# Second cross attention: high and low halves of the queries as one operand, division moved to the output

## The reference, cut to what matters

```
def _L1_xattn_ref(query, key):          # query: layernorm(x), (8, 64, 512); key: ctx_4096, (8, 1601, 512)
    a = jnp.einsum('bqd,bkd->bqk', query, key)
    e = jax.nn.softmax(a, axis=-1)
    c = jnp.einsum('bqk,bkd->bqd', e, key)
    return c
x = x + _L1_xattn_ref(_layernorm(x, axis=-1), ctx_4096)
```

## Time and profile before

| | |
|---|---|
| median of 3 runs | 2887.26 us (2886.32 to 2887.83) |
| the profiled execution | 2885.73 us |
| its span, first to last instruction | 2883.7 us |
| mean granted clock of PE | 0.957 |
| PE busy | 2637.2 us (91%) |
| DVE busy | 1934.6 us (67%) |
| ACT busy | 1477.2 us (51%) |
| POOL busy | 1457.2 us (51%) |
| the changed stage | from about 2414 to 2618 us of the span |

### The profile page before, as it was taken

The page is one execution under the profiler, slowest core; times in us unless marked ns, Lnnn a source line. Parts: engine busy times, 40 slices in busy tenths (PEclk is TensorE's granted clock), DMA queues, the critical chain, the costliest instruction groups (busy, mean ns, idle before and its releaser), DMA issues. The chain is left out here.

```text
span 2883.7 us, 43660 instructions
## 1 busy us (share of the span) xinstructions
PE 2637.2 (91%) x17160; PEld 2395.3 (83%) x17160; DVE 1934.6 (67%) x2229; ACT 1477.2 (51%) x2614; POOL 1457.2 (51%) x960
## 2 busy tenths in 40 slices
PE   7999999999999999999999999989846676996788
PEld 6899999999999999999999999978722245774677
DVE  3266776676677677667766776665559996775773
ACT  3455655555566556556555655554344433442552
POOL 2344744654644555463474474320039942785752
PEclk9999999999999999999999999999959997997879
DMA  5311110110110111011011110015140003442100
GB/s 199 132 46 31 52 53 23 60 46 30 46 60 25 36 57 42 25 51 60 23 53 48 35 53 23 25 64 179 63 151 0 0 15 110 148 133 77 49 1 15
DMA packets 92982, 168.67 MB, mean 58 GB/s; under 512 B 8514, under 2 KB 57922, under 8 KB 90234
## 3 DMA queue, kind: packets, MB, share of 16 engines
q1 hardware_dynamic: 82186, 153.75, 15.9%
q10 hardware_dynamic: 10608, 12.32, 1.3%
HBM read 146.05 MB, written 19.73 MB: 57 GB/s over the span
## 5 line engine op out<-in xcount | busy, mean ns | idle before, releaser
L355 POOL TENSOR_TENSOR xa_pt_lo<-xa_st,xa_pt_hi 128x1024 fp32r<-128x1024 f32 x255 | 510.9, 2029 | 630.1 <-ACT xa_pt_hi L534 630.1
L54 PE MATMUL xa_kv_ps<-ctx_wv_hi,ctx_hi 128*128 128x256 f32 (+1 forms) x1664 | 472.7, 284 | 3.1 <-DVE xa_v_lo L614 3.1
L56 PE MATMUL xa_kv_ps<-ctx_wv_hi,ctx_lo 128*128 128x256 f32 (+1 forms) x1664 | 469.3, 282 | 0.0
L55 PE MATMUL xa_kv_ps<-ctx_wv_lo,ctx_hi 128*128 128x256 f32 (+1 forms) x1664 | 464.8, 279 | 0.0
L54 PE MATMUL xa_kv_ps<-ctx_hi,ctx_wk_hi 128*128 128x402 f32 (+1 forms) x1024 | 362.9, 354 | 2.2 <-DVEq L688 2.2
L56 PE MATMUL xa_kv_ps<-ctx_hi,ctx_wk_lo 128*128 128x402 f32 (+1 forms) x1024 | 353.7, 345 | 0.0
L55 PE MATMUL xa_kv_ps<-ctx_lo,ctx_wk_hi 128*128 128x402 f32 (+1 forms) x1024 | 353.4, 345 | 0.0
L614 DVE TENSOR_TENSOR xa_v_lo<-xa_kv_ps,xa_v_hi 128x512 fp32r<-128x512 f32 (+1 forms) x224 | 146.3, 653 | 264.7 <-ACT xa_v_hi L507 263.7
L54 PEld LDWEIGHTS xa_kv_ps<-ctx_wv_hi,ctx_hi 128*128 128x128 f32 (+1 forms) x1664 | 305.6, 184 | 4.2 <-DVE xa_v_lo L614 3.3
L55 PEld LDWEIGHTS xa_kv_ps<-ctx_wv_lo,ctx_hi 128*128 128x128 f32 (+1 forms) x1664 | 307.8, 185 | 0.8
L56 PEld LDWEIGHTS xa_kv_ps<-ctx_wv_hi,ctx_lo 128*128 128x128 f32 (+1 forms) x1664 | 306.1, 184 | 0.0
(11 more groups left out here) (396 smaller groups left out, 6952.3 us busy)
## 6 DMA issues: line engine op xcount, KB each, us to landing
ca_nat<-in_ctx SPq DMA_DIRECT2D x48, 512.0 KB, 4.7
ctx_raw<-in_ctx_t SPq DMA_DIRECT2D x24, 804.0 KB, 6.7
ctx_wk_raw<-in_xa_wk SPq DMA_DIRECT2D x64, 256.0 KB, 2.8
ctx_wv_raw<-in_xa_wv SPq DMA_DIRECT2D x32, 512.0 KB, 4.3
q_raw<-in_xa_wq SPq DMA_DIRECT2D x8, 1024.0 KB, 4.8
q_scratch<-q_q_sb ACTq DMA_DIRECT2D x8, 1024.0 KB, 4.4
xa_q_raw<-q_scratch SPq DMA_DIRECT2D x64, 128.0 KB, 2.6
o_scratch<-xa_o_sb SPq DMA_DIRECT2D x64, 128.0 KB, 1.7
```

The lines of the kernel that those rows point to most:

```text
L54: nc.tensor.matmul(out, left[0], right[0], start=first, stop=False)
L55: nc.tensor.matmul(out, left[0], right[1], start=False, stop=False)
L56: return nc.tensor.matmul(out, left[1], right[0], start=False, stop=last)
L355: nc.gpsimd.tensor_tensor(by_chunk(pt_lo, p), scored(j, p).rearrange("p g q c -> p g c q"), by_chunk(pt_hi, p).bitcast(F32), ALU.subtract) ...
```

## The change

Queries: `q_hi` and `q_lo` become one tile `q`, in which for each contraction chunk the 64 high and the 64 low columns lie side by side. A matmul with this operand of 128 stationary columns and the high half of the context yields high x high in PSUM partitions 0 to 63 and low x high in 64 to 127; a second matmul of 64 columns adds high x low to the upper part. ACT copies partitions 64 to 127 of each finished score tile to `part_sb`; DVE adds it to partitions 0 to 63 and writes `prob`. The maximum is then taken by one reduction over the 64x1601 of `prob`. The probabilities are no longer divided: the reciprocals of the sums are written to both halves of `rden`, and the 128x512 result is multiplied by them when it is copied from PSUM. PE waits for the exponential instead of the division before it transposes the probabilities.

```diff
-        q_hi, q_lo = sc.sb("q_hi", [P, 2, KC, L], F32R), sc.sb("q_lo", [P, 2, KC, L], F32R)
+        q = sc.sb("q", [P, 2, KC, 2, L], F32R)
+        part_sb = sc.sb("part", [L, 2, TILES[0][1]])
         prob = sc.sb("prob", [L, SE])
-        tmax, nmax = sc.sb("tmax", [L, NT]), sc.sb("nmax", [L, 1])
-        den, rden = sc.sb("den", [L, 1]), sc.sb("rden", [L, 1])
+        nmax = sc.sb("nmax", [L, 1])
+        den, rden = sc.sb("den", [L, 1]), sc.sb("rden", [2 * L, 2])
...
-        s_ps = sc.ps("s_ps", [L, 2, 512])
+        s_ps = sc.ps("s_ps", [2 * L, 2, 512])
...
                 for k in range(KC)[PARTS[part]]:
-                    end = product(nc, s_ps[:, t % 2, 0:w], (q_hi[:, i % 2, k, :], q_lo[:, i % 2, k, :]),
-                                  (t_hi[:, k, c:c + w], t_lo[:, k, c:c + w]), k == 0, k == KC - 1)
+                    def both():
+                        return nc.tensor.matmul(s_ps[:, t % 2, 0:w], q[:, i % 2, k].rearrange("p i l -> p (i l)"),
+                                                t_hi[:, k, c:c + w], start=k == 0, stop=k == KC - 1)
+
+                    if k == 0:
+                        both()
+                    nc.tensor.matmul(s_ps[0:L, t % 2, 0:w], q[:, i % 2, k, 0, :], t_lo[:, k, c:c + w],
+                                     start=False, stop=False)
+                    if k > 0:
+                        end = both()
...
-                    pe.wait_ge(prob_set, n + 1)
+                    pe.wait_ge(exp_set, n + 1)
...
                 if has1:
-                    for c in range(EARLY, NC):
-                        high(h, i + 1, c)
                     n = 2 * h + i + 1
+                    for kind, at, part in SCORES:
+                        if kind == "t":
+                            high(h, i + 1, at)
+                        elif part == len(PARTS) - 1:
+                            c, w = TILES[at]
+                            w = min(w, S - c)
+                            act.wait_ge(s_full, n * NT + at + 1)
+                            act.wait_ge(s_free, n * NT + at + 1)
+                            nc.scalar.activation(part_sb[:, at % 2, 0:w], s_ps[L:2 * L, at % 2, 0:w],
+                                                 ACT.Copy).then_inc(part_set, 1)
                     act.wait_ge(nmax_set, n + 1)
...
-            def maximum(h, i, t):
+            def whole(h, i, t):
                 c, w = TILES[t]
                 w = min(w, S - c)
-                dve.wait_ge(s_full, (2 * h + i) * NT + t + 1)
-                nc.vector.tensor_scalar(prob[:, c:c + w], s_ps[:, t % 2, 0:w], 1.0, None, ALU.mult, ALU.max,
-                                        accum_out=tmax[:, t:t + 1]).then_inc(s_free, 1)
-
-            def normalise(n):
+                dve.wait_ge(part_set, (2 * h + i) * NT + t + 1)
+                nc.vector.tensor_tensor(prob[:, c:c + w], s_ps[0:L, t % 2, 0:w], part_sb[:, t % 2, 0:w],
+                                        ALU.add).then_inc(s_free, 1)
+
+            def inverse(n, s):
                 dve.wait_ge(exp_set, n + 1)
-                nc.vector.reciprocal(rden[:, :], den[:, :]).then_inc(rden_set, 1)
-                dve.wait_ge(rden_set, n + 1)
-                nc.vector.tensor_scalar(prob[:, 0:S], prob[:, 0:S], rden[:, 0:1], None, ALU.mult).then_inc(prob_set, 1)
+                for at in range(2):
+                    nc.vector.reciprocal(rden[at * L:(at + 1) * L, s:s + 1], den[:, :]).then_inc(rden_set, 1)
...
-                    nc.vector.tensor_reduce(nmax[:, :], tmax[:, :], AX_X, ALU.max, negate=True).then_inc(nmax_set, 1)
+                    nc.vector.tensor_reduce(nmax[:, :], prob[:, 0:S], AX_X, ALU.max, negate=True).then_inc(nmax_set, 1)
...
-                    nc.vector.tensor_copy(c_sb[:, :], c_ps[:, :]).then_inc(c_set, 1)
+                    dve.wait_ge(rden_set, 2 * b + 2)
+                    nc.vector.tensor_scalar(c_sb[:, :], c_ps[:, :], rden[:, i % 2:i % 2 + 1], None,
+                                            ALU.mult).then_inc(c_set, 1)
```

More of the change, by code:

```diff
@@ L1779, in context_attention @@
             sc.sem(n) for n in ("s_full", "s_free", "nmax_set", "exp_set", "pt_full", "pt_hi_set", "pt_free"))
-        pv_done, rden_set, prob_set, c_set, pad_set, own = (
-            sc.sem(n) for n in ("pv_done", "rden_set", "prob_set", "c_set", "pad_set", "own"))
+        pv_done, rden_set, c_set, pad_set, own = (
+            sc.sem(n) for n in ("pv_done", "rden_set", "c_set", "pad_set", "own"))
+        part_set = sc.sem("part_set")
         x_in = [sc.sem(f"x_in{r}") for r in range(R // P)]
@@ L1948, in query @@
                 b = 2 * h + i
-                nc.scalar.activation(q_hi[:, i % 2], xt_hi[:, :, bass.ds(b * L, L)].bitcast(F32), ACT.Copy).then_inc(q_set, 1)
-                nc.scalar.activation(q_lo[:, i % 2], xt_lo[:, :, bass.ds(b * L, L)].bitcast(F32), ACT.Copy).then_inc(q_set, 1)
+                nc.scalar.activation(q[:, i % 2, :, 0], xt_hi[:, :, bass.ds(b * L, L)].bitcast(F32), ACT.Copy).then_inc(q_set, 1)
+                nc.scalar.activation(q[:, i % 2, :, 1], xt_lo[:, :, bass.ds(b * L, L)].bitcast(F32), ACT.Copy).then_inc(q_set, 1)
             def step(h, i, has1, has2):
@@ L2036, in step @@
                         elif part == len(PARTS) - 1:
-                            maximum(h, i + 1, at)
+                            whole(h, i + 1, at)
                             if at == NT // 2 and i >= 0:
@@ L2047, in step @@
                         if c == 1:
-                            normalise(n)
+                            inverse(n, (i + 1) % 2)
                         if c in (3, 5):
```

## The result

| | before | after |
|---|---|---|
| median | 2887.26 us (5 runs, 2885.41 to 2887.83) | 2934.25 us (5 runs, 2932.02 to 2938.58) |
| the profiled execution, its span | 2885.73, 2883.7 us | 2934.37, 2932.3 us |
| mean granted clock of PE | 0.957 | 0.947 |
| six batches: from the value products of the first to those of the seventh | 131.04 us | 184.87 us |

The change made the kernel 47 us slower: the ratio is 1.0165, 95% interval 1.0151 to 1.0179. I had predicted 2883.9 in a range of 2874 to 2894.

What follows compares the result with a forecast made beforehand. PE and an equally long loop through the other engines were taken to bound the kernel. First batch's scores -2.6, first to second E -1.6, six batches +1.3, tail -0.5 gave -3.4 us: 2883.9, range 2874 to 2894.

Steps and rivals of the forecast that it cites:

- part 1: Score products: one matmul fewer per contraction chunk and tile, wide weights free; PE relieved of 2.88 us a batch.
- E: The moment in a batch at which the value products start; 2501.55 in the batch read before the change.
- L: Start of the first low half of the next early transposes; forecast at E+6.27 instead of 3.84.
- part 2: Softmax chain: copy, add and one long maximum make it longer; L moves 2.43 us later, PE waits 1.98 at chunk 3.
- part 3: Division moved to the end: DVE loses a 1.05 us multiplication; L to M becomes 9.55 us, before 10.22.
- rival (b): Shared port: POOL's low halves hold DVE's group 2, 1.2 us a batch; +8 us in all, 2895, chance 0.10.
- Rival (c): PE's clock falls once a batch behind the new 2 us gap; +15 us, 2899, chance 0.07.
- The loop: One batch, E to E', through the other engines, taut together with PE; forecast 22.05 us against 21.84.
- M: Start of the low half of chunk 7; forecast at L+9.55, before 10.22.
- E': The next batch's E; forecast 6.23 us after M instead of 7.66.
- the tail: The stretch after the last E, said to be set by POOL; forecast -0.5 us (-3 to +1.5).
- Rival (a): PE stays the bound, removed matmuls worth their time: 23 us, 2864; partial form 2879; chance 0.23, nearly all partial.

Runs made afterwards that it cites:

- Joined only: The kernel after with the division back in its old place, ahead of the probabilities' transposes: 2937.29 us, ratio to before 1.018.
- division only: The kernel before with the division moved to the output and nothing else: 2929.21 us, ratio to before 1.0145.
- pool waits: The kernel after, but POOL starts its row of four low halves only after DVE's low half of group 1: 2890.16 us, ratio to before 1.0012.
- before late: The kernel before with only DVE's low half of the context's group 1 moved behind the low halves of the probabilities: 2925.56 us, ratio to before 1.0137.
- the filler: pool waits plus 18 matmuls whose result nobody reads, in PE's gap at chunk 3: 2889.28 us, ratio to before 1.0009.
- reordered: The kernel after; ACT's query copies and two high halves precede its wait for the maximum, DVE does low 0, 1, then both context low halves: 2874.53 us, ratio 0.9958.
- DVE early: The kernel after with DVE's low halves of context groups 0 and 1 directly after the maximum, before the early low halves: 2895.26 us, ratio to before 1.0025.
- one at a time on before: The kernel before, old products kept, with ACT's new order and DVE's context low halves separated, after low 0 and low 2: 2900.25 us, ratio to before 1.0047.

## Why the prediction was wrong

**Right, by its own steps.** In the kernel after, score products of both kinds start 0.18 us apart, 32 a batch, the wide weights cost nothing (part 1). In the batch with E = 2548.06, one of three in which PE idles for 1.9 us ahead of chunk 3 (1.7 to 1.8 in the others), the last add is at E+0.92 (forecast E+0.96), the maximum takes 1.81 (1.82), the exponential starts at E+3.36 (3.42), L is E+6.35 (6.27), chunk 3 at E+7.09 after 1.92 us of idle PE (7.02, 1.98). ACT's copy is 0.50 and DVE's add 0.56, as worked out (part 2). The first batch's scores take 8.9 us instead of 11.4 (-2.5, forecast -2.6). From the first E (2435.37) to the second it is 20.75 instead of 23.16 (-2.4, forecast -1.6), and there the number is nearer than its parts: the next scores start at +11.6 (forecast +11.0) and take 9.1 (10.6), since the clock was back at 1.00 when they started, where I had added 0.8 for a longer slow stretch. The maximum was not held by POOL in any batch: 1.81 beside its copies.

**Wrong: part 3, and with it rival (b).** The step said that POOL's copies "are released later too", so that the row of four low halves starts at about L+7.4. It starts at L+6.1 (2499.66 - 2493.56). I moved POOL's last copies by PE's gap at chunk 3, but not the earlier ones, which are done by then: three are left behind L instead of five. And I had counted that POOL's copies hold DVE, but not that DVE's multiplication and low halves held POOL's, four copies in 6.70 us. Joined only and division only show the two causes apart. POOL's row came 2.1 us earlier against L (8.22 to 6.1), DVE's group 1 only 0.1 us (5.89 to 5.76). The 2.3 us between the two starts became 0.34. The forecast had 7.4 and 5.34, so 2.1 us between them: the row was 1.3 us too late in it, and group 1 was 0.4 us too early, because its sister, group 0, met a copy as well and took 1.87 instead of 1.21.

The second half of the failure is the price. I let a held DVE instruction wait "for the end of POOL's instruction" and gave the rival 1.2 us a batch. It waits for three instructions: 6.5 us more than the 1.89 of before, a PE gap of 6.3, and the half clock behind it. The row that I cited for the price, and as agreeing with the rule that one instruction keeps the pair, already spoke against it: 5.68 for an addition of 0.69 is 5.0 us of waiting, beside a row of four POOL instructions that lasted 8.65 (2600.79 to 2609.44), 2.2 us each. That is more than two of them, and I didn't divide.

Rival (b) was thus the right mechanism at the wrong instruction (group 1, not group 2) with a fifth of its price; pool waits (taken out: -44 us), before late and division only (put in: +38 and +42) show it from both sides. Part 3's own bound for L+6.9, "7.6 (both `n_lo` held)", allowed for copies as the holder only.

**Rival (c), the clock, was half right.** The gap of 2 us at chunk 3 does lower it, but not in every batch: with pool waits in four of six, about 1 us each, 4.0 us in the stage by the filler. Its price of 15 us was too high. Where the gap is 6.3 us it falls each time.

**The loop without the collision** is 22.48 as a mean over the six batches with the filler, against my 22.05. The part from L to M was too short by 0.3: 9.85 instead of 9.55, with the low half of chunk 6 at L+7.14 instead of 6.9. L itself is E+6.35 (forecast 6.27) and from M to E' it is 6.28 (6.23). Chunk 10 waits 0.92 as a mean (forecast 0.9).

**The account.** Six batches +53.8, the first batch -2.5 - 2.4, the tail +1.0 (25.06 instead of 24.08; my -0.5 was wrong in sign, and the cause was not traced): +49.9. The two spans differ by 48.6. The other -1.3 is the sum of two stretches: up to the first scores the profiled execution of after is 3.2 us later, and behind the last `c_sb` it is 4.5 us shorter. Neither was explained.

**Rival (a) came true only after reordering.** The prediction held that the removed matmuls turn into waits because the softmax chain delays L, and so it is in after and pool waits. But that delay was a matter of order: ACT's query copies and two high halves can stand under the maximum. With that, and DVE's low halves one at a time, 2.1 of the 2.88 us a batch arrive.

## What to carry over

Before taking work off DVE, list its instructions with two SBUF operands, see how far each stands from POOL's rows, and recompute both starts: here 0.44 us of room was what the kernel before lived on, and removing 1 us of DVE work cost 42. Divide any held duration by that of one instruction of the engine that holds, to see whether the hold ends with that instruction or lasts over several. And a saving on the bounding engine arrives only once the chains around it are put in an order that lets it, so try the change together with its order.

## What was not expected of the hardware

- DVE's low half of the context, which reads two SBUF operands, was kept out over the boundaries of POOL's back-to-back instructions: 8.1 to 8.4 us instead of 1.2, let in only ahead of the fourth of four (2506.60 above), though it had been started 0.34 us before the first, while the last of POOL's copies was still under way. The Trainium skill (SBUF — State Buffer, Who interferes with whom) names the shared port pair and says that the engine that issues first keeps it "for the whole instruction". By that rule the wait would end at 2502.0, at the first boundary at the latest; the trace has 2506.6, and the measurement decides. Why the first two boundaries didn't let it in stays open. In every hold here, from before the row or from 1.1 us into it (before late), DVE came in ahead of the fourth, which is both the last of the row and the smallest; no run separates the two.
- The hold goes both ways. With three of POOL's copies in the way DVE's pair took 3.67 to 3.96 us, and POOL's three copies took 4.67 (2502.15 in reordered) instead of 3 x 1.05.
- A PE gap of 1.9 us amid full work lowered the clock in four of six batches (pool waits), one of 2.9 in all six (DVE early), one of 1.35 in four of six (one at a time on before), one of 1.25 in none (reordered).
- Weights of 128 columns beside 64, in front of 402 moving columns, changed no distance between matmuls: 0.18 us for both kinds.
